# A state-space mixer on five engines: one softplus step moved from GpSimd to VectorE, and TensorE's small jobs re-slotted

## The reference

```python
x_ = einsum('ed,bld->bel', in_proj_w, context)          # 512 channels
u  = silu(depthwise_conv(x_, conv_w) + conv_b)          # 4 taps
dt_lo, Bm, Cm = split(einsum('ke,bel->bkl', x_proj_w, u))
delta = softplus(dt_proj_w @ dt_lo + dt_proj_b)
state = state * exp(delta * A) + (delta * u) * B_t      # scan over 512 positions, 16 states
y_t = sum_n state * C_t ;  y = (y + D * u) * silu(layernorm(x))
x = x + y
logits = layernorm(x) @ gate_kernel                     # 8 experts, top 2
x = x + experts(layernorm(x))                           # gated FFN, 1024 wide
```

## Time and profile before

| what | us |
|---|---|
| median of 3 runs | 1330.68 (1323.72, 1330.68, 1347.05) |
| the profiled execution's own time | 1325.02 |
| its span in the trace | 1322.3 |
| set-up, until GpSimd's first multiplication by B | 0 to 53.9 |
| mixer, until VectorE's last multiplication by C | to about 555 |
| the mixer's tail: last gating, normalisation, logits | to 586 |
| routing and experts | 586 to 1322 |
| busy in the span: TensorE, VectorE, GpSimd, ScalarE | 1124.1, 751.0, 639.7, 526.0 |

### The profile page before, as it was taken

One profiled execution on the slowest core, in us unless ns is written; L12 is line 12 of the kernel. 1 busy time (PEld: TensorE's weight loads), 2 busy tenths in 40 slices (PEclk: granted clock), 3 DMA queues, 4 the chain that ended last, 5 costly groups with the idle time before them and its releaser, 6 DMA issues.

```text
span 1322.3 us, 19385 instructions
## 1 busy us (share of the span) xinstructions
PE 1124.1 (85%) x4940; PEld 837.2 (63%) x4940; DVE 751.0 (57%) x815; ACT 526.0 (40%) x707; POOL 639.7 (48%) x472
## 2 busy tenths in 40 slices
PE   4667988788868877833999999999999999999994
PEld 2234555446444645533788888888888888888883
DVE  3789899887998699837324353442532534324321
ACT  3775655674667464322213232321321323213210
POOL 0399899898989799613023222321222322213221
PEclk8587777686878577855999999999999999999998
DMA  5333232522242224045314243242421524314310
GB/s 180 123 102 103 67 119 88 167 78 91 75 158 82 88 75 156 1 145 204 137 48 167 97 152 125 87 154 76 171 96 48 174 104 160 104 46 174 103 40 25
DMA packets 65445, 145.08 MB, mean 110 GB/s; under 512 B 8655, under 2 KB 11215, under 8 KB 65409
## 3 DMA queue, kind: packets, MB, share of 16 engines
q1 hardware_dynamic: 56368, 116.34, 25.9%
q0 software_dynamic: 9040, 28.32, 6.5%
HBM read 320.53 MB, written 18.35 MB: 256 GB/s over the span
## 4 chain that ended last, share of the span: by engine, by line
PE 52%; DVE 2%; DMA 1%; issue 0%; POOL 0%; ACT 0%; POOLq 0%; DVEq 0%
PE hp L1423 11%; PE hp L1422 10%; PE hp L1421 10%; PE yp L1421 5%; PE yp L1423 5%; PE yp L1422 5%; PE tp L1462 2%; PE xp L1415 1%; PE hp L1406 1%; PE yp L1470 1%; DMA work<-xln_dram,index 0%; DMA work<-out_dram,acc_index 0%; DMA out_dram<-work,out_index 0%; DVE R L1288 0%; POOL index L1034 0%
## 5 line engine op out<-in xcount | busy, mean ns | idle before, releaser
L266 POOL TENSOR_TENSOR ring<-du,bB 128x1024 f32<-128x1024 f32 x128 | 299.3, 2357 | 75.5 <-DVE du L610 52.4
L539 DVE TENSOR_TENSOR_SCAN ring<-dA,ring 128x512 f32<-128x512 f32 x256 | 295.7, 1202 | 17.7 <-ACT dA L349 11.1
L349 ACT ACTIVATE dA<-delta,Acol 128x512 f32<-128x512 f32 x256 | 172.3, 687 | 170.4 <-DVE ring L539 168.0
L1421 PE MATMUL hp<-w_hi,xT_hi 128*128 128x512 f32 x592 | 236.4, 399 | 0.9 <-DVE xT_lo L1318 0.9
L1423 PE MATMUL hp<-w_hi,xT_lo 128*128 128x512 f32 x592 | 236.3, 399 | 0.0
L1422 PE MATMUL hp<-w_lo,xT_hi 128*128 128x512 f32 x592 | 234.1, 395 | 0.0
L682 PEld LDWEIGHTS yT<-ident,ring 128*128 128x128 f32 x1024 | 146.7, 172 | 97.3 <-issue 76.9
L663 PE MATMUL Cb<-xdbl,ident 48*128 48x512 f32 x176 | 126.9, 808 | 87.9 <-DVE ring L545 87.8
L682 PE MATMUL yT<-ident,ring 128*128 128x128 f32 x1024 | 172.9, 332 | 10.7 <-POOL ring L275 10.7
L1339 DVE TENSOR_TENSOR work<-hp,work 128x512 f32<-128x512 f32 x74 | 51.1, 690 | 229.3 <-PE hp L1423 226.2
L1058 POOL COPY out_index<-out_tab 128x1 uint32 x37 | 6.7, 181 | 355.0 <-DVE work L1325 355.0
(11 more groups left out here) (180 smaller groups left out, 1408.6 us busy)
## 6 DMA issues: line engine op xcount, KB each, us to landing
stage<-in_L_ffn_w_kernel_dram SPq DMA_DIRECT2D x160, 1024.0 KB
stage<-in_L_ffn_wo_kernel_dram SPq DMA_DIRECT2D x78, 1024.0 KB
bB<-bcs SPq DMA_DIRECT2D x64, 512.0 KB, 3.6
bC<-bcs SPq DMA_DIRECT2D x40, 256.0 KB, 4.4
xall<-in_x_dram SPq DMA_DIRECT2D x1, 4096.0 KB, 14.8
xln_dram<-xlnb SPq DMA_DIRECT2D x4, 1024.0 KB, 6.9
out_dram<-xall SPq DMA_DIRECT2D x4, 1024.0 KB, 9.1
ctx_rows<-in_ctx_dram SPq DMA_DIRECT2D x4, 512.0 KB, 5.5
```

Source lines behind the costliest of these rows:

```text
L266: g_.tensor_tensor(ring[:, q % RING, :].rearrange("p (e l) -> p e l", e=2), dub(b, h * 2 * L, 2 * L).rearrange("p (e l) -> p e l", e=2), B ...
L349: a_.activation(dA[r % SB][:, :], db(b, eb * L, L), ACT.Exp, scale=Acol[:, eb, n:n + 1]).then_inc(exp_done, 1)
L539: v_.tensor_tensor_scan(o, dA[r % SB][:, :], o, 0.0, ALU.mult, ALU.add).then_inc(scan_done, 1)
L1421: t_.matmul(bank[:, :], a_hi[:, k, :], b_hi[:, b, :], start=(start and k == ks[0]), stop=False)
```

## The change

Four things change, all in the order of the mixer's work; no operation is added or left out.

1. `sub_loss` goes from GpSimd to VectorE, at steps 4 (half 1 of the batch) and 26 (half 0 of the next). GpSimd's `add_ln` and `times_u` move up: `add_ln` from step 11 to 9 and from 30 to 29, `times_u` from 13 to 11; the other `times_u` stays at 31.
2. The logits of batches 0 and 1 are no longer made at step 31 of the batch after, but at step 1 of the one after that, with VectorE's copy at step 3. Those of batch 2 are made at step 26 of batch 3 and copied at step 30; the transposes for them move from step 28 to 20.
3. `in_proj` is cut into four single steps (4 and 5 or 8 and 9, then 12 and 13).
4. `ctx_T` for batch 3 moves from step 0 to 5, `zs_T` of batches 1 to 3 from steps 3 and 6 to 6 and 7, with ScalarE's copies to match.

```diff
@@ GpSimd
-            def sub_loss(b, i):
-                pool.wait_ge(soft_loss, b * 2 + i + 1)
-                pool.wait_ge(relu_done, b * 2 + i + 1)
-                d = db(b, i * 2 * L, 2 * L)
-                g_.tensor_tensor(d, d, dub(b, i * 2 * L, 2 * L), ALU.subtract).then_inc(soft_sub, 1)
...
                     if s == 9:
-                        sub_loss(b, 1)
+                        add_ln(b, 1)
                     if s == 11:
-                        add_ln(b, 1)
-                    if s == 13:
                         times_u(b, 1)
...
-                    if s == 28 and b + 1 < NB:
-                        sub_loss(b + 1, 0)
-                    if s == 30 and b + 1 < NB:
+                    if s == 29 and b + 1 < NB:
                         add_ln(b + 1, 0)
@@ ScalarE
-                    if s == 3 and nxt:
+                    if s == (6 if b > 1 else 3) and nxt:
                         ctx_T(b + 1)
...
-                    if s == 6 and rest:
+                    if s == 7 and rest:
                         zs_T(b, (0, 1))
...
-                    if s == 31 and rest:
+                    if s == (30 if nxt else 22) and rest:
                         gate_T(b - 1, 2)
@@ VectorE
+            def sub_loss(b, i):
+                dve.wait_ge(soft_loss, b * 2 + i + 1)
+                dve.wait_ge(relu_done, b * 2 + i + 1)
+                d = db(b, i * 2 * L, 2 * L)
+                v_.tensor_tensor(d, d, dub(b, i * 2 * L, 2 * L), ALU.subtract).then_inc(soft_sub, 1)
...
+                    if s == 4:
+                        sub_loss(b, 1)
+                    if s == 3 and b > 1:
+                        logit_copy(b - 2)
...
-                if rest and nxt:
-                    logit_copy(b - 1)
+                    if s == 26 and nxt:
+                        sub_loss(b + 1, 0)
+                    if s == 30 and rest and not nxt:
+                        logit_copy(b - 1)
...
-            logit_copy(NB - 2)
@@ TensorE
-                    if s == 0 and nxt:
+                    if s == 1 and b > 1:
+                        logits_of(b - 2)
+                    if s == (5 if b > 1 else 0) and nxt:
                         ctx_T(b + 1)
-                    if s == 3 and rest:
+                    if s == 6 and rest:
                         zs_T(b, (0, 1))
-                    if s == 6 and rest:
+                    if s == 7 and rest:
                         zs_T(b, (2, 3))
...
                     if s == 8 and nxt and rest:
-                        in_proj(b + 1, (0, 1))
+                        in_proj(b + 1, (0,))
+                    if s == 9 and nxt and rest:
+                        in_proj(b + 1, (1,))
...
-                    if s == 28 and rest:
+                    if s == (28 if nxt else 20) and rest:
                         gate_T(b - 1, 2)
                         gate_T(b - 1, 3)
-                    if s == 31 and rest:
+                    if s == 26 and rest and not nxt:
                         logits_of(b - 1)
```

More of the change, by code:

```diff
@@ L772, in _ @@
                         acc(q - LAG)
-                    if s == 0 and nxt:
+                    if s == 1 and b > 1:
+                        logits_of(b - 2)
+                    if s == (5 if b > 1 else 0) and nxt:
                         ctx_T(b + 1)
-                    if s == 3 and rest:
+                    if s == 6 and rest:
                         zs_T(b, (0, 1))
-                    if s == 6 and rest:
+                    if s == 7 and rest:
                         zs_T(b, (2, 3))
                     if s == 4 and nxt and not rest:
-                        in_proj(b + 1, (0, 1))
+                        in_proj(b + 1, (0,))
+                    if s == 5 and nxt and not rest:
+                        in_proj(b + 1, (1,))
                     if s == 8 and nxt and rest:
-                        in_proj(b + 1, (0, 1))
+                        in_proj(b + 1, (0,))
+                    if s == 9 and nxt and rest:
+                        in_proj(b + 1, (1,))
                     if s == 9 and not rest:
@@ L787, in _ @@
                     if s == 12 and nxt:
-                        in_proj(b + 1, (2, 3))
+                        in_proj(b + 1, (2,))
+                    if s == 13 and nxt:
+                        in_proj(b + 1, (3,))
                     if s == 16 and rest:
```

## The result

| | before | after |
|---|---|---|
| median of 19 runs each | 1325.63 us | 1331.31 us |
| lowest and highest run | 1323.06, 1347.05 | 1326.66, 1333.55 |
| ratio of after to before | | 1.0036, 95% interval 1.0022 to 1.005 |
| profiled execution, own time and span | 1325.02, 1322.3 | 1331.31, 1329.6 |
| last gating of the mixer starts at | 560.97 | 567.69 |

The change costs a third of a per cent, some 5 us. That is inside the range of the prediction, and within what was called no change, but the interval excludes the gain of 9.5 us that the sum gave. The ratio leaves out the four executions of the kernel before that took 1345 us or more, a slower state of the chip. The profiled executions differ by 6.3 us, and all of it is there when the last gating starts (6.7 us later): the experts are not touched, so the mixer is the place to read.

A forecast was written before the change was run, and what follows sets the result against it. VectorE's queue, with its waits for TensorE, was taken as the mixer's pace; +10.5 - 5.0 - 17.7 + 6.5 + 2.5 - 2.2 - 0.6 + 0.5 - 4.0 = -9.5 us against 1325.0 gave 1315.5, range 1299 to 1332.

The forecast's parts named there:

- waits for Cb (+6.5 + 2.5 - 2.2 - 0.6): VectorE's waits for TensorE's broadcast of C: logits at step 1, at step 26, projection split, context transposes moved.
- That VectorE's queue, not GpSimd's, is the pace: Mixer from 82 us on: VectorE's queue, with its waits for TensorE, reaches the end last; GpSimd is ahead.
- The rival at 1290: GpSimd sets the mixer's pace, so its removed work and waits come off whole: -35 us; chance 0.17.
- The subtraction, +10.5: VectorE, steps 4 and 26: moved subtractions plus longer losses at step 25 add 10.5 us, bounds +6.7 and +14.2.
- +0.63 per overlap: Added time of a VectorE subtraction or loss that meets a busy GpSimd, 0.63 us each.
- What an earlier GpSimd is worth, -5.0: VectorE's waits at the normalisation, 235.44 and 495.00, shrink as GpSimd's rstd steps come sooner; bounds -5.6 and -3.0.
- The logits, -17.7 + 6.5 + 2.5: Batch ends: both copy stalls go, -17.7 us; new waits cost +6.5 at step 1, +2.5 at batch 3's step 26.
- 8 us at step 4: Sign: a Cb wait near 8 us at step 4 of batches 2 and 3 would mean the clock decided.
- the third rival: Waits only move from the logits to Cb; only the tail's 4 us remain: 1321 us; chance 0.18.
- the second, given 0.15: Rival: TensorE at 1.2 GHz makes logits and z transposes ahead of Cb cost double: +8.7, 1333.7 us; chance 0.15.
- The projection and z, -2.2 and +0.5: Split projection shortens batch 0's Cb waits, -2.2 us; later z transposes cost ScalarE's copies in three batches, +0.5.
- The tail, -4.0: Mixer's end: batch 2's logits no longer precede the last two units' transposes; -4.0 us, bounds -4.3 and -2.0.

The follow-up runs named there:

- p234_jobs: Kernel after with the subtraction back on GpSimd at its old steps; 1322.89 us, ratio 0.996 to the kernel before.
- p34_small_jobs: Kernel before with projection split and z transposes at steps 6 and 7, logits unmoved; 1321.97 us, 0.9941; run again 1321.64 us, 0.996.
- sub_one_later: Kernel before with GpSimd's subtraction for the next batch's first half at step 29, not 28; 1327.53 us, ratio 0.9992.
- p1_subtraction: Kernel before with only the subtraction moved to VectorE and GpSimd's steps moved up; 1332.8 us, ratio 1.0058.
- logits_next_batch: Kernel after with the subtraction back on GpSimd and batch 2's logits back at step 31 of batch 3; 1323.63 us, ratio 0.9988.
- proj_split: Kernel before with only the input projection cut into single steps; 1326.65 us, ratio 1.0018.
- extra_two_inputs: Kernel before with 16 added VectorE additions of two SBUF tiles, results unused; 1369.31 us, no ratio given.
- quarters_guess_later: Kernel after with subtraction back on GpSimd, logits in quarters, and ScalarE's guess_2 at step 10, not 9; 1313.54 us, ratio 0.9895.
- z_later: Kernel before with only the z transposes at steps 6 and 7, ScalarE's copies at 7 and 8; 1334.98 us, 1.0059; again 1336.68, 1.0082.

## Why the prediction was right or wrong

The forecast's terms beside the account of the two profiled executions (us):

| term | forecast | account |
|---|---|---|
| subtraction and longer losses | +10.5 | +16.4 |
| stalls of the logits' copies | -17.7 | -17.5 |
| waits for Cb (+6.5 + 2.5 - 2.2 - 0.6) | +6.2 | +10.7 |
| waits for exponentials (-5.0 + 0.5) | -4.5 | +1.8 |
| waits for the taps | in the bounds only | +3.0 |
| waits for GpSimd | 0 | -4.1 |
| the tail | -4.0 | -3.0 |
| small gaps; earlier start of the mixer | 0 | +1.3; -1.85 |
| sum | -9.5 | +6.7 |

By experiments, which hold over many executions: part 1 had +10.5 - 5.0 = +5.5 and measured +7.7, +10 and +12.7; the logits' moves had -17.7 + 6.5 + 2.5 - 4.0 = -12.7 and measured 0 to +2.5 (p234_jobs against the two results of p34_small_jobs). So the logits are the larger miss, and the subtraction the smaller; part 1 taken back gives a gain (0.996), and the logits cut in pieces give no loss (0.9991).

**That VectorE's queue, not GpSimd's, is the pace: right.** In the kernel after VectorE waits 2.5 us for GpSimd, GpSimd's own waits grew, as the prediction said they would, and sub_one_later shows that less waiting on GpSimd brings nothing. The rival at 1290 falls.

**The subtraction, +10.5: wrong in size.** Forecast were 1.75 at step 4, 1.12 at step 26 and +0.63 for each of three losses at step 25. The subtractions came out close (10.3 us in all, two of the seven long: 1.75 and 2.32). The losses did not: those at step 25 took 2.37, 2.40 and 2.41 us and two at step 3 took 3.29 and 3.07. The failed step is "+0.63 per overlap": the three losses at step 25 cost +3.6, not +1.9, and those at step 3, for which the sum had no term, a further +3.1 (15.9 - 9.2 - 3.6). I had taken one row, 193.77, as the price of an overlap; it was the price of an overlap that began 0.7 us before GpSimd's instruction ended. The rows of the kernel after show the rule that holds here. GpSimd and VectorE at three places, with a row of each in turn:

```profile
197.01 5.65 POOL L266 TENSOR_TENSOR ring<-du,bB 128x1024 f32<-128x1024 f32 x2
198.12 2.32 DVE L559 TENSOR_TENSOR delta<-delta,du 128x1024 f32<-128x1024 f32 x1
...
320.87 2.35 POOL L275 TENSOR_TENSOR ring<-ring,bC 128x1024 f32<-128x1024 f32 x1
321.01 3.29 DVE L553 SCALAR_TENSOR_TENSOR du<-spw,spy 128x1024 f32<-128x1024 f32 x1
323.19 3.34 POOL L266 TENSOR_TENSOR ring<-du,bB 128x1024 f32<-128x1024 f32 x1
...
414.52 2.34 POOL L266 TENSOR_TENSOR ring<-du,bB 128x1024 f32<-128x1024 f32 x1
415.54 2.41 DVE L553 SCALAR_TENSOR_TENSOR du<-spw,spy 128x1024 f32<-128x1024 f32 x1
```

Who starts first is not slowed at all (2.35 and 2.34 us, its time alone). The other ends 1.08 to 1.09 us after the first one's end: 320.87 + 2.35 = 323.22, and the loss ends at 324.30; 414.52 + 2.34 = 416.86, and it ends at 417.95. At 197.01, where two GpSimd instructions are merged, the first ends at 199.36 by its 2.35, the subtraction at 200.44. And GpSimd's next one then ends 2.23 us after the loss (324.30, 326.53). So the two do not share, they take turns. The earlier trace rows obey it too: the loss ended at 195.60, GpSimd's next at 197.83. This agrees with the Trainium skill, SBUF — State Buffer, its part "SBUF: two separate sides", which calls the port pair an exclusive lock, held for the whole instruction by whichever starts first; I had used only the page that names a contention. So, as an estimate from these rows, an instruction of 1.2 us that starts anywhere in a busy GpSimd's row of 2.35 us costs 1.2 to 3.4 us, with 2.3 in the middle, and GpSimd a further 1.0. The long rows are not all part 1's doing: p234_jobs, with the subtraction on GpSimd, has a loss of 3.27 us at 193.52.

**What an earlier GpSimd is worth, -5.0: the waits went, the gain did not stay.** The waits at 235.44 and 495.00 are gone in the kernel after. But ScalarE's exponentials are waited for elsewhere (2.60 us at 80.29, 2.10 at 484.33, and 2.47 at 353.02), 12.9 us in all against 11.1. Two causes can be told apart. In p1_subtraction, where nothing else moves, these waits fell to 7.5 us; the rest came with the other parts. And in batch 0 the wait for GpSimd of 3.51 us went, but at that place the kernels with part 1 wait 2.60 us for the exponential and over 3 for the next Cb, as VectorE's timeline of p1_subtraction shows:

```profile
82.30 2.34 DVE L529 TENSOR_TENSOR_SCAN ring<-dA,ring 128x512 f32<-128x512 f32 x2 [2.60 <-ACT dA L339]
88.02 1.23 DVE L535 TENSOR_TENSOR ring<-Cb,ring 128x1024 f32<-128x1024 f32 x1 [3.39 <-PE Cb L663]
```

**The logits, -17.7 + 6.5 + 2.5: wrong in size, the larger miss.** The stalls went as forecast (0.2 us are left). Their price was taken at half, "about half, +6.5". All three blocks met 1.2 GHz, and 3.10 + 3.59 + 6.63 us of waits for Cb stand directly behind them (at the second place there were 1.22 before). The prediction named 8 us at step 4 as the sign that the clock decides; it was 3.1 and 3.6 there, and its full price only at step 26 (6.63 of the 6.9 that were the upper end). And -17.7 was itself the stall of one profile in which both blocks ran slow; in p34_small_jobs it is 3.47 each, in most others 9 to 12 for the two. Measured, the move of the logits (with the context's transposes) is worth nothing to a slight loss (p234_jobs and logits_next_batch against p34_small_jobs). That the waits only move was the third rival; that the blocks at 1.2 GHz make it slower the second, given 0.15, and its 1333.7 is the nearest to the 1331.3 measured. The nearness of that number is in part luck: it too took the subtraction at +10.5 where 16.4 was found, and it put +13.4, +6.9 and +6.6 on TensorE's places, 26.9 in all, where the waits for Cb, exponentials and taps grew by 15.5 together.

**The projection and z, -2.2 and +0.5: wrong by interaction.** Together they gain 0.4 to 0.6% (5 to 8 us), one by one they do nothing and lose 0.6 to 0.8%. In the whole change one sees some of their costs. The taps on VectorE wait 3.0 us (2.8 in proj_split, none before). The Cb wait of batch 0, from which -2.2 was to come, is 3.10 us at 85.73 (1.25 before), but that is part 1's, as the row at 88.02 above shows; in proj_split it is 1.22, so the split left it as it was, while the other one (1.65 at 112.73) is gone there. And ScalarE waits for z and starts the two table loads of its normalisation behind the copies; VectorE then waits for the exponential behind them, as the timelines of the kernel after show:

```profile
346.15 0.60 ACT L329 ACTIVATE zsT<-pp 128x512 f32<-128x512 f32 x1 [5.56 <-PE pp L724]
...
350.48 1.28 ACT L412 ACT_TABLE_LOAD   x1
...
353.02 2.34 DVE L529 TENSOR_TENSOR_SCAN ring<-dA,ring 128x512 f32<-128x512 f32 x2 [2.47 <-ACT dA L339]
```

**The tail, -4.0: nearly right**, 3.0; 3.02 us of wait for the last transposes remain, at a granted clock of 0.64.

**The method.** The sum was right in its path and in most of its signs, and missed by 16 us, in several terms that mostly leaned one way. An overlap was priced from one favourable row, a stall from one unfavourable execution, and the price of the blocks at half, although it hangs on the clock that they meet. What made the miss no larger was partly chance and partly a gain that was hardly forecast: an earlier start of 1.85 us, and 5 to 8 us from the small moves.

## What to carry to other kernels

A VectorE instruction with two SBUF inputs beside a GpSimd that is seldom idle cost its own time plus what was left of GpSimd's instruction, and it charged GpSimd's next one 1 us. Work of that form moved from GpSimd to VectorE took 16.5 us from the engine that was not the pace and put 13.5 to 17.0 on the one that was; and an idle GpSimd beside such an instruction was worth 1.2 us for each loss. A long block of low priority in front of an operand that another engine waits for should be cut into pieces, not moved whole: the same products in quarters gained 0.65 to 1.0% over the kernel that has them whole (0.45% with part 1), where the moves of the whole blocks gained nothing clear of noise. And a stall read from one profile, where TensorE's clock goes up and down, should be priced at both levels before it is put in a sum at the one that was seen.

## What the runs showed of the hardware that was not expected

**One VectorE instruction can lose the turn several times.** In extra_two_inputs an addition that takes 1.21 us alone took 12.34. GpSimd's and VectorE's timeline of that kernel:

```profile
108.01 4.70 POOL L267 TENSOR_TENSOR ring<-du,bB 128x1024 f32<-128x1024 f32 x2
110.66 12.34 DVE L568 TENSOR_TENSOR spare<-u 128x1024 f32<-128x1024 f32 x1
112.65 2.36 POOL L276 TENSOR_TENSOR ring<-ring,bC 128x1024 f32<-128x1024 f32 x1
114.95 6.97 POOL L267 TENSOR_TENSOR ring<-du,bB 128x1024 f32<-128x1024 f32 x3
```

GpSimd's instructions follow each other without a gap and unstretched to 121.92, and the addition ends 1.08 us later, at 123.00. It began inside the second of the two at 108.01, which ended at 112.71, and let four more pass. Of the other fifteen additions one met an idle GpSimd (1.21 us), and fourteen got their turn at the first end, as at the three places above.

It is no freak of the added instructions. In the long execution of quarters_guess_later the loss of batch 1 shows the same, with four more instructions passing it after the one at 192.21:

```profile
192.69 12.15 DVE L563 SCALAR_TENSOR_TENSOR du<-spw,spy 128x1024 f32<-128x1024 f32 x1
...
201.43 2.33 POOL L266 TENSOR_TENSOR ring<-du,bB 128x1024 f32<-128x1024 f32 x1
210.53 2.37 POOL L275 TENSOR_TENSOR ring<-ring,bC 128x1024 f32<-128x1024 f32 x1 [6.77 <-DVE ring L539]
```

The loss ends at 204.84, 1.08 us after GpSimd's last one (203.76), and GpSimd then stands idle until VectorE's next scan; in extra_two_inputs it stands idle as well (3.41 us, until 125.33). So in both cases VectorE got its turn only when GpSimd had nothing left that it could do without VectorE. In all other profiles no such instruction took over 3.5 us. What makes VectorE miss its turn is open.

**The products of the logits seldom meet the full clock.** A block of 32 rows with 8 columns took 6.83 us in all three places of the kernel after, 5.05 to 6.83 in most others, and 3.64 in a few, in kernels that hardly differ; the time of one and the same kernel falls into groups some 10 us or more apart (z_later: 1318 to 1322 and 1333 to 1339). No run shows which comes first, the clock or the schedule; a missed turn as above is of the same size (9 to 11 us), but it was caught in two profiles only, so that it makes the groups is not shown.
